# Turned probabilities of a cross-attention kernel: hand-over copies issued by two engines instead of one, in 32 KB pieces

## The reference

```python
q = split_heads(x @ w_q, 20)                      # x: 8 x 1024 x 640, heads of 32
k, v = split_heads(text @ w_k), split_heads(text @ w_v)        # 56 text tokens of 1024
k_ip, v_ip = split_heads(ip @ w_k_ip), split_heads(ip @ w_v_ip)  # 8 image tokens
out = softmax(q k / sqrt(32)) v + softmax(q k_ip / sqrt(32) + mask_ip) v_ip
out = merge_heads(out) @ w_out + b_out + x
```

## Time and profile before

| | us |
|---|---|
| median of 2 runs | 876.94 (876.62 to 877.26) |
| the profiled execution | 873.89 |
| its span, first to last instruction | 872.1 |
| mean granted clock of TensorE, share of full speed | 0.976 |

### The profile page before, as it was taken

How to read it: one execution, slowest core, us unless ns; L and a number is a source line. 1 busy time by engine, 2 the same in 40 slices (tenths; PEclk the granted TensorE clock), 3 DMA queues, 4 the chain that set the end, 5 groups by cost and what they waited for, 6 DMA issues and landing times.

```text
span 872.1 us, 13091 instructions
## 1 busy us (share of the span) xinstructions
PE 814.0 (93%) x4381; PEld 650.9 (75%) x4381; DVE 670.6 (77%) x983; ACT 541.3 (62%) x928; POOL 624.1 (72%) x576
## 2 busy tenths in 40 slices
PE   9999779999989998999989998999989998998586
PEld 8899558787868776787868776887867786885464
DVE  7758578888868796888868796888868796987853
ACT  7766267675766666665656666667757666675531
POOL 0069349696959786787959786887959697887841
PEclk9999989999999999899999999999999999999898
DMA  9933343536362725446462726445463626252525
GB/s 324 378 94 119 108 126 89 176 115 187 113 194 52 232 57 165 143 120 181 120 192 57 225 55 182 130 127 170 133 192 100 191 88 212 58 177 62 176 61 193
DMA packets 138867, 128.08 MB, mean 147 GB/s; under 512 B 17072, under 2 KB 101040, under 8 KB 138672
## 3 DMA queue, kind: packets, MB, share of 16 engines
q1 hardware_dynamic: 138656, 125.93, 48.4%
q10 hardware_dynamic: 144, 1.31, 0.4%
HBM read 61.32 MB, written 23.59 MB: 97 GB/s over the span
## 4 chain that ended last, share of the span: by engine, by line
SPq 45%; DVE 17%; PE 15%; DMA 11%; issue 7%; ACT 4%; POOL 1%; ACTq 0%; DVEq 0%
SPq L462 39%; DMA xin<-in_xT 6%; DVE res L962 4%; SPq L497 4%; DVE xT_lo L117 3%; PE bank L100 3%; DVE stage L237 3%; PE bank L101 3%; PE bank L102 3%; DMA res<-in_xT 2%; DVE o_raw L956 2%; DMA prob<-stage 2%; PE bank L196 1%; ACT xT_hi L113 1%; DVE top L216 1%
## 5 line engine op out<-in xcount | busy, mean ns | idle before, releaser
L573 POOL TENSOR_TENSOR pT_lo<-prob,pT_hi 128x512 fp32r<-128x512 f32 x80 | 116.4, 1455 | 99.9 <-ACT pT_hi L720 99.6
L725 ACT ACTIVATE pv_part<-bank 64x512 f32<-64x512 f32 x160 | 94.7, 592 | 148.2 <-PE bank L1167 145.8
L249 POOL TENSOR_TENSOR prob<-prob,top 128x896 f32<-128x896 f32 (+1 forms) x160 | 179.4, 1142 | 4.5 <-DVE top L216 4.1
L256 POOL TENSOR_TENSOR prob<-prob,inv 128x896 f32<-128x896 f32 (+1 forms) x160 | 172.6, 1101 | 11.3 <-DVE inv L224 10.6
L100 PE MATMUL bank<-oT_hi,wo_hi 128*128 128x512 f32 x400 | 168.9, 422 | 8.3 <-POOL oT_lo L569 4.7
L100 PE MATMUL bank<-xT_hi,wq_hi 128*128 128x512 f32 x400 | 156.0, 390 | 5.8 <-ACT qT L139 3.2
L101 PE MATMUL bank<-oT_lo,wo_hi 128*128 128x512 f32 x400 | 159.1, 398 | 0.0
L102 PE MATMUL bank<-oT_hi,wo_lo 128*128 128x512 f32 x400 | 158.6, 396 | 0.0
L101 PE MATMUL bank<-xT_lo,wq_hi 128*128 128x512 f32 x400 | 155.6, 389 | 0.0
L102 PE MATMUL bank<-xT_hi,wq_lo 128*128 128x512 f32 x400 | 155.6, 389 | 0.0
L569 POOL TENSOR_TENSOR oT_lo<-o_raw,oT_hi 128x512 fp32r<-128x512 f32 x80 | 109.9, 1374 | 61.9 <-ACT oT_hi L729 60.6
(11 more groups left out here) (103 smaller groups left out, 1247.8 us busy)
## 6 DMA issues: line engine op xcount, KB each, us to landing
prob<-stage SPq DMA_DIRECT2D x512, 64.0 KB, 2.0
res<-in_xT SPq DMA_DIRECT2D x16, 1280.0 KB, 9.3
outT<-res SPq DMA_DIRECT2D x80, 256.0 KB, 2.6
xin<-in_xT SPq DMA_DIRECT2D x15, 1280.0 KB, 6.3
prob<-stage SPq DMA_DIRECT2D x256, 32.0 KB, 1.9
w_raw<-in_L_xattn_w_k SPq DMA_DIRECT2D x8, 320.0 KB, 4.9
w_raw<-in_L_xattn_w_k_ip SPq DMA_DIRECT2D x8, 320.0 KB, 5.3
w_raw<-in_L_xattn_w_v_ip SPq DMA_DIRECT2D x8, 320.0 KB, 4.3
```

The source lines that it names most:

```text
L249: ins = nc.gpsimd.tensor_tensor(s, s, top[:, m, n, :].unsqueeze(2).broadcast_to([P, ROWS, k1 - k0]), ALU.subtract)
L256: ins = nc.gpsimd.tensor_tensor(s, s, inv[:, m, n, :].unsqueeze(2).broadcast_to([P, ROWS, k1 - k0]), ALU.mult)
L573: nc.gpsimd.tensor_tensor(pT_at(pT_lo, g, p), pT(p), pT_at(pT_hi, g, p).bitcast(F32), ALU.subtract).then_inc(pT_lo_pool, 1)
```

## The change

The sixteen DMAs of a hand-over are issued for each chunk by itself, as soon as that chunk is turned: eight by SyncE (destination quadrants 0 and 1) and eight by ScalarE (2 and 3). That is 80 DMAs of 32 KB to a group in place of 48, 40 on each of the two engines. `stage` and `prob` are laid out so that the 256 elements which one DMA carries to a partition are one run of 1 KB on both sides. ScalarE issues its halves at set places of its order: chunk 4 of `g` after `oT_part(g, 1)`; chunks 0 and 1 of the next group after `move_pv(g, 7)`, ahead of `pT_part(g, 8)`; chunks 2 and 3 after `pT_part(g+1, 3)`, which puts them ahead of the fifth `move_q`. The ring `stage` has three slots instead of four, used in turn, and each chunk has its own landing semaphore. The loads of `x` and of the residual are five DMAs each instead of one, `x` for `g+3` is loaded at the head of the iteration, and a piece of the residual waits only for the store of its own piece. The rounded and rest parts of the probabilities read `prob` in four runs of 128 elements.

```diff
-S_RING = 4
+S_RING = 3
...
-        SHARES = ((0, 2), (2, 4), (4, 5))
-        pT_landed = [sem(f"pT_landed{i}") for i in range(len(SHARES))]
+        pT_landed = [sem(f"pT_landed{m}") for m in range(KD)]
...
+        def hand_over(eng, g, m, quads):
+
+            n = KD * g + m
+            eng.wait_ge(turned, n + 1)
+            wait(eng, pT_landed[m], 16 * QUADS * QUADS * g)
+            for c in quads:
+                for q in range(QUADS):
+                    eng.dma_start(prob[c * QUAD:(c + 1) * QUAD, m * CHUNK:(m + 1) * CHUNK].rearrange("i (q f) -> i q f", q=QUADS)[:, q, :],
+                                  stage[q * QUAD:(q + 1) * QUAD, n % S_RING, c].rearrange("i h t -> i (h t)")).then_inc(pT_landed[m], 16)
+
+        SP_QUADS, ACT_QUADS = range(2), range(2, QUADS)
...
         def turn(dve, g, m):
 
-            before = (g, 3) if m == 4 else (g - 1, 4) if m == 3 else (g - 1, m)
-            dve.wait_ge(prob_done, KD * g + m + 1)
-            if before[0] >= 0:
-                landed(dve, *before)
-            src = prob[:, m * CHUNK:(m + 1) * CHUNK].rearrange("p (t c i) -> p t c i", t=GT, i=QUAD)
-            dst = stage[:, stage_slot(m)].rearrange("p c (t i) -> p t c i", i=QUAD)
+            n = KD * g + m
+            dve.wait_ge(prob_done, n + 1)
+            if n >= S_RING:
+                landed(dve, *divmod(n - S_RING, KD))
+            src = prob[:, m * CHUNK:(m + 1) * CHUNK].rearrange("p (t h c i) -> p t h c i", t=GT, h=2, i=QUAD)
+            dst = stage[:, n % S_RING].rearrange("p c h (t i) -> p t h c i", i=QUAD)
             nc.vector.transpose(dst, src).then_inc(turned, 1)
...
         def pT(p):
 
-            return prob[:, p * GQ:(p + 1) * GQ]
+            m, h = divmod(p, 2)
+            return prob[:, m * CHUNK:(m + 1) * CHUNK].rearrange("p (q h t) -> p q h t", q=QUADS, h=2)[:, :, h, :]
...
                 for g in range(NG):
                     b = g // GPB
-                    hand_over(g, 2)
+                    if g + 3 < NG:
+                        load_x(g + 3)
                     if g > 0:
                         for m in OUT_ORDER:
                             store(g - 1, m)
+                    hand_over(sp, g, 4, SP_QUADS)
+                    for m in OUT_ORDER:
+                        load_res(g, m)
                     if g % GPB == 0 and b < B - 1:
                         sp.wait_ge(k_built, HPT * (b + 1))
                         load_k(sp, b + 1)
                         load_v(b + 1)
                     if g + 1 < NG:
-                        hand_over(g + 1, 0)
-                    if g + 3 < NG:
-                        load_x(g + 3)
-                    load_res(g)
-                    if g + 1 < NG:
-                        hand_over(g + 1, 1)
+                        for m in range(KD - 1):
+                            hand_over(sp, g + 1, m, SP_QUADS)
...
                     pT_part(g, 7)
                     oT_part(g, 1)
+                    hand_over(act, g, 4, ACT_QUADS)
                     if more:
                         exponentials(act, n, 0)
...
                     move_pv(g, 7)
+                    if more:
+                        hand_over(act, n, 0, ACT_QUADS)
+                        hand_over(act, n, 1, ACT_QUADS)
                     pT_part(g, 8)
                     pT_part(g, 9)
...
                     if more:
                         pT_part(n, 3)
+                        hand_over(act, n, 2, ACT_QUADS)
+                        hand_over(act, n, 3, ACT_QUADS)
```

More of the change, by code:

```diff
@@ L168, in attention_kernel @@
             sem(n) for n in ("mask_added", "max_subbed", "prob_done", "pT_lo_pool", "oT_lo_done"))
-        res_loaded, stored = sem("res_loaded"), sem("stored")
-        SHARES = ((0, 2), (2, 4), (4, 5))
-        pT_landed = [sem(f"pT_landed{i}") for i in range(len(SHARES))]
+        res_loaded, stored = [sem(f"res_loaded{m}") for m in range(KD)], [sem(f"stored{m}") for m in range(KD)]
+        pT_landed = [sem(f"pT_landed{m}") for m in range(KD)]
         def landed(eng, g, m):
-            share = min(m // 2, len(SHARES) - 1)
-            wait(eng, pT_landed[share], 16 * QUADS * QUADS * (g + 1))
+            wait(eng, pT_landed[m], 16 * QUADS * QUADS * (g + 1))
+        def hand_over(eng, g, m, quads):
[7 more added lines that the diff above has]
+        SP_QUADS, ACT_QUADS = range(2), range(2, QUADS)
         SPANS = ((0, NTEXT), (NTEXT, KEYS))
@@ L280, in attention_kernel @@
         v_parts = sb("v_parts", [P, PAIRS, 2, HP], F32R)
-        stage = sb("stage", [P, S_RING, 2 * QUADS, P])
+        stage = sb("stage", [P, S_RING, QUADS, 2, P])
         ctxT_hi, ctxT_lo = ctxT[:, :, 0, :], ctxT[:, :, 1, :]
@@ L386, in pT, with pT_part_at @@
         def pT(p):
-            return prob[:, p * GQ:(p + 1) * GQ]
+            m, h = divmod(p, 2)
+            return prob[:, m * CHUNK:(m + 1) * CHUNK].rearrange("p (q h t) -> p q h t", q=QUADS, h=2)[:, :, h, :]
         def pT_at(t, g, p):
             return t[:, (PAIRS * g + p) % P_RING, :]
+        def pT_part_at(t, g, p):
+            return pT_at(t, g, p).rearrange("p (q t) -> p q t", q=QUADS)
         def oT_at(t, g, m):
@@ L452, in _, with load_res @@
                     load_chunk(c)
[L454 to L463, removed]
                 def load_x(g):
                     sp.wait_ge(xT_lo_done, KD * (g - 1))
[L467 to L473, removed]
+                    for k in range(KD):
+                        sp.dma_start(x_of(g)[:, k, :], x_half[g % 2, g // 2][:, k, :]).then_inc(x_loaded[g % 2], 16)
+                def load_res(g, m):
+                    wait(sp, stored[m], 16 * g)
+                    sp.dma_start(res[:, m, :], x_half[g % 2, g // 2][:, m, :]).then_inc(res_loaded[m], 16)
+                hand_over(sp, 0, 0, SP_QUADS)
+                hand_over(sp, 0, 1, SP_QUADS)
                 sp.wait_ge(v_ip_added, 2)
@@ L496, in store @@
                     sp.wait_ge(out_done, outs_before(g, m) + 1)
-                    sp.dma_start(out_half[g % 2, g // 2, m], res[:, m, :]).then_inc(stored, 16)
+                    sp.dma_start(out_half[g % 2, g // 2, m], res[:, m, :]).then_inc(stored[m], 16)
                 load_x(2)
-                hand_over(0, 1)
+                hand_over(sp, 0, 2, SP_QUADS)
+                hand_over(sp, 0, 3, SP_QUADS)
                 sp.wait_ge(v_text_ready, 3 * BLOCKS // 2)
@@ L516, in _ @@
                     if g + 1 < NG:
-                        hand_over(g + 1, 0)
-                    if g + 3 < NG:
-                        load_x(g + 3)
-                    load_res(g)
-                    if g + 1 < NG:
-                        hand_over(g + 1, 1)
+                        for m in range(KD - 1):
+                            hand_over(sp, g + 1, m, SP_QUADS)
                 for m in OUT_ORDER:
                     store(NG - 1, m)
-                sp.wait_ge(stored, 16 * KD * NG)
+                for m in range(KD):
+                    sp.wait_ge(stored[m], 16 * NG)
             @block.gpsimd
@@ L719, in pT_part @@
                     wait(act, pv_ready, PAIRS * g + p + 1 - P_RING)
-                    nc.scalar.activation(pT_at(pT_hi, g, p), pT(p), ACT.Copy).then_inc(pT_hi_done, 1)
+                    nc.scalar.activation(pT_part_at(pT_hi, g, p), pT(p), ACT.Copy).then_inc(pT_hi_done, 1)
                 def move_pv(g, p):
@@ L732, in split_x @@
                     if k == 0:
-                        act.wait_ge(x_loaded[g % 2], 16 * (g // 2 + 1))
+                        act.wait_ge(x_loaded[g % 2], 16 + 16 * KD * (g // 2))
                         act.wait_ge(q_ready, KD * g)
@@ L742, in v_hi_part @@
                         nc.scalar.activation(v_head(v_parts, 0, j), v_own(j), ACT.Copy).then_inc(v_hi_built, 1)
+                hand_over(act, 0, 0, ACT_QUADS)
+                hand_over(act, 0, 1, ACT_QUADS)
                 v_hi_part(0)
@@ L749, in _ @@
                     pT_part(0, p)
+                hand_over(act, 0, 2, ACT_QUADS)
+                hand_over(act, 0, 3, ACT_QUADS)
                 move_q(act, 1, 3)
@@ L958, in output @@
                 def output(g, m):
-                    dve.wait_ge(res_loaded, 16 * (g + 1))
+                    dve.wait_ge(res_loaded[m], 16 * (g + 1))
                     dve.wait_ge(out_ready, outs_before(g, m) + 1)
```

6 lines of the change are left out of this document (2 added, 4 removed).

## The result

The changed kernel takes 1176.59 us (1174.17 to 1179.0, 2 runs) against 876.94: a ratio of 1.341, 95% interval 1.3355 to 1.3466. The profiled execution took 1174.17 us, its span is 1172.4. The forecast was slower, 1109 us, with a range up to 1165.

A forecast was written before the change was run, and what follows sets the result against it. TensorE was taken as nearly the bound, losing 28.4 us to late probabilities behind SyncE's issues. 873.9 + 222.6 (fourteen periods, 15.9 each) + 8 + 5 - 4 = 1105.5 profiled; the median 3 above, 1109 us; range 945 to 1165.

The forecast's parts named there:

- Price of an issue: ScalarE's 40 issues a group: each takes 0.64 us of ScalarE's time, like the old hand-over, 25.6 us together.
- both stops named: TensorE, behind ScalarE's bursts: idle 8 us before pair 8 and 8 us before a group's first scores.
- In the first stretch ScalarE then always has work, but for waits that remain: ScalarE, `move_pv(g, 2)` to fifth `move_q`: 24.3 work, 25.6 issues, only 1.4 us of waits and gaps.
- the second stretch: ScalarE, end of the fifth `move_q` to the next `move_pv(g, 2)`: 12.4 us, its idle end no room for earlier issues.
- The wait for the turn of chunk 4: ScalarE after `oT_part(g, 1)`: it still waits 0.6 us until VectorE has turned chunk 4.
- 8 - 4: Last groups: +8 us for iteration 14's bursts, -4 for group 15's last chunk, handed over by eight issues, not sixteen.
- Ten load pieces for two: `x` and residual loads: 8 more issues on SyncE cost nothing, as long as SyncE has slack.
- The three slots: Ring `stage`: a turn waits for the chunk three back, issued earlier, costing nothing; late landings would hold VectorE.
- The earlier landings are inside the 11.1 us already spent: Earlier landings gain at most ScalarE's 77.2 us of waiting, already counted in its 11.1 us idle time a period.
- Cheap issues: Rival, chance 0.30: 1 KB runs make issues cheaper, 973 us at 0.34 us each, 1038 at 0.49.
- each other's way: Rival, chance 0.06: only one engine issues at a time, each pays 1.28 us an issue, about 1480 us.
- Hiding: Rival, chance 0.14: issues fit before pair 8; below 0.15 us each 839 us, up to 0.25 within 2%.

The follow-up runs named there:

- e_price: Kernel before plus, behind its end, nine DMA forms issued by SyncE, then ScalarE, then both together; medians 590 to 632 ns SBUF to SBUF, 421 to 470 with one DRAM end.
- e_dose: Kernel before, hand-overs unchanged, plus 40 useless 16 B-a-partition DMAs a group issued by ScalarE at the change's three places; 1121.15 us, ratio 1.279.
- e_late_c: Changed kernel with ScalarE's burst of sixteen for chunks 2 and 3 moved from ahead of the fifth move_q to behind oT_part(g, 0); 1072.37 us, ratio 1.225.
- e_late_a: Changed kernel with ScalarE's burst of eight (chunk 4) moved behind the first move_q of the next but one group; 1156.30 us, ratio 1.319.
- e_dose_w: Kernel before with e_dose's 40 useless ScalarE issues a group, and ahead of every eight a wait for the turned chunk, as in the change; 1157.17 us, ratio 1.321.
- e_runs: Kernel before with only the change's layout (1 KB runs on both sides), SyncE alone, 48 DMAs, four slots; 874.09 us, ratio 0.998.

## Why the prediction was right in direction and short in size

**Price of an issue.** Right: 613 ns on ScalarE. The row chosen, the old hand-over, was the right one, and `e_price` shows why: the two ends in SBUF set the price.

**Where ScalarE's time stands.** Right: both stops named, 7.66 and 6.73 us, forecast at 8 each. `e_dose` and `e_late_c` bear the mechanism out.

**The step that failed** is "In the first stretch ScalarE then always has work, but for waits that remain", with 1.4 us for them. Its sum, 24.3 + 25.6 + 1.4 + 12.4 = 63.7, came out as follows in the period shown. The stretch of 54.85 us holds 25.4 of work, 26.2 of issues (5.65 + 10.43 + 0.51 + 9.61) and so 3.3 that are left (4.7 of idle time, less 1.4 in which issues ran beside an instruction); the other stretch is 13.0. The period is 67.9, over the loop 67.7 (first scores at 123.33 and at 1070.76, fourteen groups on). The error of 4.2 is thus 1.1 of work (this period has the keys to build, mine had not), 0.6 of issues, 1.9 of waits, 0.6 of the second stretch. The next period, 610.32 to 678.64, builds no keys, like mine: of its 68.3 us, 24.4 are work, 26.8 issues, 4.1 are left, and 13.0 are the second stretch. So the waits are the largest part: 3.3 to 4.1 us net, where the sum had 1.4.

Behind the waits stands what I left out: I listed two bursts that TensorE waits for. The first burst, of eight, delays `move_q(x, 0)`, so TensorE stops a third time, 44.0 us in all; it is then late with pair 6, for which ScalarE waits in turn (1.03 us), and ScalarE waits for GpSimd ahead of the fourth exponential (1.46 us). `e_late_a` shows the size: moved behind that `move_q`, the burst costs 20 us less. The wait for the turn of chunk 4 was priced rightly, 0.6 us against 0.64; but such waits make 36 us in `e_dose_w`, against the 9 that fifteen times 0.6 give, about half of which comes from the burst no longer beginning beside the instruction ahead of it (19 us, above).

Fourteen periods of 4.0 us make 56 of the 69 us by which the profiled time, 1174.2, exceeds 1105.5. The rest lies at the two ends, where I had small terms of the same kind. First scores of group 1 and last group's scores in the kernel before:

```profile
112.99 1.16 PE L196 MATMUL bank<-k_diag,qT 64*128 64x128 f32 x16
...
781.95 1.16 PE L196 MATMUL bank<-k_diag,qT 64*128 64x128 f32 x16
```

and in the changed kernel:

```profile
123.33 2.08 PE L204 MATMUL bank<-k_diag,qT 64*128 64x128 f32 x16 [6.43 <-ACT qT L139]
...
1070.76 2.08 PE L204 MATMUL bank<-k_diag,qT 64*128 64x128 f32 x16 [7.56 <-ACT qT L139]
```

The loop starts 10.3 us later, not 5: the first burst ahead of it took 14.15 us and not the 10.2 that fit, and behind the second, half of which I had let an old stall take, TensorE waits 6.43 us for the `move_q`. From the last row to the end of the span there are 101.6 us, before 90.2: 11.4 more where I had 8 - 4.

**The edits at nothing.** Layout: right (`e_runs`). Ten load pieces for two: right only under the condition that I gave, slack on SyncE, which waits 332.6 us for turns in the changed kernel; without it they cost 48 us. The three slots were not tried alone, but the trace of the changed kernel answers: VectorE is idle ahead of none of its 80 turns, so it never waited for a slot. "The earlier landings are inside the 11.1 us already spent": consistent, not separately shown.

**The rivals.** Cheap issues and each other's way are ruled out by `e_price`, and by the 613 ns of ScalarE's issues in the changed kernel itself. Hiding: 24 issues of 0.65 us cost 51 us, 40 cost 244, so the slack is there but small; the price below 0.15 us an issue that this rival needed does not occur.

**The last 20 us**, between `e_dose_w` and the change, can mostly be read from the two traces. `e_dose_w` has no burst ahead of its loop, and its first scores of group 1 start 11 us before the changed kernel's 123.33:

```profile
112.37 1.16 PE L196 MATMUL bank<-k_diag,qT 64*128 64x128 f32 x16
```

Fourteen groups on the distance is 17.9 us (1052.87 and 1070.76), and it is the same at the end of the spans. The 7 us that are added within the loop are of the size of the issues' own difference, 613 ns in the median against 602, over 560 issues some 6 us (an estimate). Small landings or the two halves of a hand-over ending apart could at most make what little remains; neither was tried alone.

## What to carry to other kernels

A queue that is moved to a compute engine costs that engine its issue time, and the page does not count it as busy: add issues times price to the engine's order, and ask of each burst what stands directly behind it. Idle time of an engine in a tight loop is room only at its own place; cut the period at the points where the other engine waits, and list every consumer behind every insertion, since the one left out here was worth 20 us. Before more engines are given to a late transfer, look at what stands ahead of it in its own queue: moving stores and loads behind the urgent share gave 4%, while the split cost 34%.

## What the runs showed of the hardware

- In the nine forms of `e_price` the time of an issue goes by where the two ends lie: 590 to 632 ns SBUF to SBUF, 421 to 470 with one end in DRAM (back to back; 318 to 378 for the fastest of each eight), and 16 B or 1 KB a partition make no difference (590 and 592 ns on SyncE, 612 and 612 on ScalarE). ScalarE pays 8 to 22 ns more than SyncE.
- The first issue of a burst need not wait for the instructions ahead of it: one started at 586.48, while `move_q` ran (586.33, for 0.60) and before `pT_part`, which also stands ahead of it, had started (586.83). What stands behind the burst waits for its end (issues until 596.63, the next instruction at 596.68).
- TensorE's clock after a stop. Two windows of the changed kernel follow (stretch, length, busy of PE, PEld, DVE, ACT, POOL, then the granted clock). Behind a stop of 6.73 us the score unit and the next matmuls ran at a granted 0.50, the lower of the two levels (1.2 GHz); in the second window the mean is 0.93.

```profile
597.33:600.50 3.17, 3.17 (x19) 2.75 (x20) 2.27 (x4) 3.10 (x6) 0.00 (x0) 0.50 0.75 258
601.00:609.66 8.66, 8.66 (x36) 7.04 (x36) 5.43 (x9) 2.67 (x5) 3.71 (x4) 0.93 0.09 36
```

The unit took 2.08 us there and 1.16 at the higher level (at 781.95 in the kernel before, shown above, where the granted clock was 1.00). So a stop can cost more than its length. That this is part of why the last 16 issues cost 13 us a group and not 10.4 fits TensorE's busy time, 57 us longer, but was not tried alone.
